# Graph attention on one core: two heads' target rows by VectorE turns and DMA, and their maxima a slot sooner

## What is computed

```python
xl = (x @ W).reshape(B, N, H, F)
asrc = jnp.einsum('bnhf,hf->bnh', xl, a_src)
adst = jnp.einsum('bnhf,hf->bnh', xl, a_dst)
e = jax.nn.leaky_relu(asrc[:, :, None, :] + adst[:, None, :, :], NEG_SLOPE)
e = jnp.where(mask[..., None], e, NEG_INF)
attn = jax.nn.softmax(e, axis=1)
out = jnp.einsum('bsdh,bshf->bdhf', attn, xl)
```

## Time and profile before

| | |
|---|---|
| median of 3 runs | 887.39 us (885.66 to 888.89) |
| the profiled execution | 883.62 us |
| its span, first to last instruction | 881.7 us |
| PE busy | 839.4 us (95%) |
| DVE busy | 745.3 us (85%) |
| ACT busy | 692.9 us (79%) |
| POOL busy | 277.0 us (31%) |
| mean granted clock of TensorE | 0.992 |

### The profile page before, as it was taken

How to read it: one execution, slowest core, us unless ns; L and a number is a source line. 1 busy time by engine, 2 the same in 40 slices (tenths; PEclk the granted TensorE clock), 3 DMA queues, 4 the chain that set the end, 5 groups by cost and what they waited for, 6 DMA issues and landing times.

```text
span 881.7 us, 17000 instructions
## 1 busy us (share of the span) xinstructions
PE 839.4 (95%) x5996; PEld 788.6 (89%) x5996; DVE 745.3 (85%) x1922; ACT 692.9 (79%) x1302; POOL 277.0 (31%) x244
## 2 busy tenths in 40 slices
PE   6798989999999999999999999999999999999896
PEld 4688879999999999999999999899999999889675
DVE  6868797979798888979888896988889798897766
ACT  2677869788796978879697887969788796979563
POOL 0002020233343333334333333433333343334222
PEclk9899999999999999999999999999999999999999
DMA  9123131322313131231423123042312301200002
GB/s 250 55 73 73 48 96 50 96 49 55 93 47 97 68 101 50 70 96 32 93 70 99 49 57 111 26 98 72 96 49 56 106 33 25 72 1 2 24 1 72
DMA packets 100379, 59.81 MB, mean 68 GB/s; under 512 B 66244, under 2 KB 84804, under 8 KB 100296
## 3 DMA queue, kind: packets, MB, share of 16 engines
q1 hardware_dynamic: 100296, 58.73, 24.6%
HBM read 41.82 MB, written 8.50 MB: 57 GB/s over the span
## 4 chain that ended last, share of the span: by engine, by line
PE 75%; DVE 11%; ACT 8%; issue 3%; another core or an unknown queue 0%; POOL 0%; DMA 0%; SPq 0%; POOLq 0%; DVEq 0%; ACTq 0%
PE bUU L558 19%; PE bUU L580 11%; PE bUU L569 10%; PE bG L652 10%; PE bG L670 9%; PE bG L640 4%; PE bB L518 3%; DVE junk L1010 3%; PE bUU L548 2%; ACT att L787 2%; DVE att L1010 2%; PE bG L667 2%; DVE att L1057 1%; PE bA L518 1%; ACT att L802 1%
## 5 line engine op out<-in xcount | busy, mean ns | idle before, releaser
L558 PE MATMUL bUU<-val,att 128*128 128x129 f32 x2048 | 249.5, 275 | 1.3 <-DVE att L1061 1.3
L558 PEld LDWEIGHTS bUU<-val,att 128*128 128x128 f32 x2048 | 240.2, 192 | 2.9 <-issue 1.9
L1061 DVE SCALAR_TENSOR_TENSOR att<-mask_n,att 128x2048 f32<-128x2048 bf16 x64 | 148.5, 2320 | 74.8 <-ACT att L802 69.8
L787 ACT ACTIVATE att<-bB,val 128x512 f32<-128x512 f32 x320 | 204.1, 716 | 5.2 <-PE bB L518 5.2
L802 ACT ACTIVATE att<-att 128x2048 f32<-128x2048 f32 x64 | 123.7, 1933 | 0.6
L426 POOL TENSOR_SCALAR var_eps<-moments 128x4 f32<-128x4 f32 x29 | 29.9, 1032 | 299.1 <-DVE moments L1103 299.1
L1010 DVE CUSTOM_DVE_ANT_0 junk<-mask_t,a_rows,val 128x512 bf16<-128x512 bf16 x168 | 121.8, 778 | 0.0
L569 PE MATMUL bUU<-val,att 128*128 128x257 f32 x480 | 113.1, 385 | 5.1 <-DVE att L1057 4.0
L580 PE MATMUL bUU<-val3s,att 128*128 128x256 f32 x480 | 108.3, 379 | 0.2 <-DVE res L1091 0.2
L1010 DVE CUSTOM_DVE_ANT_0 junk<-mask_t,bA,val 128x512 bf16<-128x512 bf16 x152 | 104.1, 740 | 4.2 <-PE bA L518 4.2
L569 PEld LDWEIGHTS bUU<-val,att 128*128 128x128 f32 x480 | 87.7, 190 | 21.9 <-DVE att L1057 5.4
(11 more groups left out here) (128 smaller groups left out, 1690.5 us busy)
## 6 DMA issues: line engine op xcount, KB each, us to landing
adj_in<-in_adj_dram SPq DMA_DIRECT2D x16, 1024.0 KB, 5.8
a_rows<-a_rows_dram SPq DMA_DIRECT2D x56, 256.0 KB, 3.8
x_in<-in_x_dram SPq DMA_DIRECT2D x16, 512.0 KB, 6.7
out_dram<-act SPq DMA_DIRECT2D x14, 512.0 KB, 2.9
mask_t<-mask_n SPq DMA_TRANSPOSE x64, 2.5
a_rows_dram<-val SPq DMA_DIRECT2D x56, 2.0 KB
att<-in_L_gnn_W_dram SPq DMA_DIRECT2D x4, 128.0 KB, 3.3
val<-in_L_gnn_W_dram SPq DMA_DIRECT2D x1, 512.0 KB, 7.4
```

The lines of the kernel that those rows point to most:

```text
L558: ins = nc.tensor.matmul(to[:, (d % 2) * FX:(d % 2 + 1) * FX], p[:, s, d * P:(d + 1) * P], val1[u.batch % 2][:, s, u.index // 2, values], ...
L787: nc.scalar.activation(p[:, b], bB[:], ACT.Prelu, bias=a_col(u, b), alpha=SLOPE)\
L1061: nc.vector.scalar_tensor_tensor(flat(p), mask_n[u.batch % 3][:, 0:NB * N], BIG, flat(p), ALU.add, ALU.min)\
```

## The change

Four things are changed, all for the heads 2 and 3 of batches 2 to 15 (28 heads):

- Their targets' terms no longer pass through TensorE and `bB`. VectorE writes them to every eighth column of `b_wide` (128x32), turns that in 32x32 blocks into `b_turned`, and SP stores the turned rows to DRAM and reads them back as a row onto 128 partitions (`spread_targets`): head 2's into `a_rows[:, 3]`, free once head 3's source row has been copied to `bA`, head 3's into a new tile `b_rows`. ScalarE's `leaky` reads these rows in SBUF.
- VectorE also turns the sources' scores of the next batch (`turn_scores`, position 2), and `store_scores` writes runs of 32 elements instead of single ones.
- `tops` and `shifted_targets` of head 2 move from position 2 to position 1, behind `keep_edges` of head 0; those of head 3 from position 3 to position 2.
- GpSimd waits for head 2's new semaphore before `add_bias_2`.

```diff
+            def spread_targets(n, i):
+                sp.wait_ge(b_turned_ready, 2 * (n - 2) + i + 1)
+                if n > 2:
+                    sp.wait_ge(b_spread[i], 16 * (n - 2))
+                sp.dma_start(b_dram[i].rearrange("(b q i) -> q b i", b=NB, i=32),
+                             b_turned[0:P:32 // NB, :]).then_inc(b_stored, 16)
+                sp.wait_ge(b_stored, 16 * (2 * (n - 2) + i + 1))
+                if i == 0:
+                    sp.wait_ge(arow_copied, n - 1)
+                elif n > 2:
+                    sp.wait_ge(leaky_done, (units[SLOTS * (n - 1) + 3 + i].u + 1) * NB)
+                sp.dma_start(b_rows[i], b_dram[i].rearrange("(o n) -> o n", o=1).to_broadcast([P, N]))\
+                    .then_inc(b_spread[i], 16)
...
                     load_x(n + 2)
+                if n >= 2:
+                    spread_targets(n, 0)
                 if 2 <= n + 1 < B:
                     store_scores(n + 1)
+                if n >= 2:
+                    spread_targets(n, 1)
+                if 2 <= n + 1 < B:
                     spread_scores(n + 1)
...
-                    pool.wait_ge(b_t_ready, units[SLOTS * n + 3].r + 1)
+                    if n >= 2:
+                        pool.wait_ge(b_turned_ready, 2 * (n - 2) + 1)
+                    else:
+                        pool.wait_ge(b_t_ready, units[SLOTS * n + 3].r + 1)
                     add_bias_2(n - 1)
...
-                if after and after.row:
+                if after and after.row and not after.targets_by_dma:
                     targets_row(after)
...
-                if u.row:
+                if u.targets_by_dma:
+                    act.wait_ge(b_spread[u.index - 2], 16 * (u.batch - 1))
+                elif u.row:
                     act.wait_ge(brow_done, u.r + 1)
...
+                if u.targets_by_dma:
+                    k = 2 * (u.batch - 2) + u.index - 2
+                    if k:
+                        dve.wait_ge(b_turned_ready, k)
+                    nc.vector.scalar_tensor_tensor(b_wide[:, 0:32:32 // NB], top[u.u % 2][:], TOP, low[:], ALU.subtract,
+                                                   ALU.min, reverse0=True).then_inc(b_wide_ready, 1)
+                    if k:
+                        dve.wait_ge(b_stored, 16 * k)
+                    dve.wait_ge(b_wide_ready, k + 1)
+                    nc.vector.transpose(b_turned[:], b_wide[:]).then_inc(b_turned_ready, 1)
+                    return
...
+            def turn_scores(n):
+                dve.wait_ge(val1_ready, (n + 1) * NB)
+                if n > 2:
+                    dve.wait_ge(a_stored, 16 * H * (n - 2))
+                nc.vector.transpose(scores_t[:], val1[n % 2][:, :, :, HC:HX]).then_inc(scores_turned, 1)
...
+                if n >= 2 and pos in (2, 3):
+                    after = units.get(g + 2) if pos == 2 else None
...
+                if pos == 2 and n + 1 < B:
+                    turn_scores(n + 1)
...
+                if pos == 1 and 2 <= n < B:
+                    tops(units[g + 2])
+                    shifted_targets(units[g + 2])
                 if pos == 1 and 0 <= n - 2 < B:
                     norm_stats(n - 2, 0, res1, res1_done, NB, stats1, moments1)
```

More of the change, by code:

```diff
@@ L36, in __init__ @@
         self.banked = self.by_dma and index == 3
+        self.targets_by_dma = self.by_dma and index >= 2
 def gat_kernel(nc, x, adj, W1, as1, ad1, b1, W2, as2, ad2, b2, W3, a3, out):
@@ L74, in gat_kernel @@
         u.u = i
-    for i, u in enumerate(u for u in units.values() if u.row):
+    for i, u in enumerate(u for u in units.values() if u.row and not u.targets_by_dma):
         u.r = i
@@ L148, in gat_kernel @@
         a_rows = sb("a_rows", [P, H, N])
+        b_wide = sb("b_wide", [P, 32])
+        b_turned = sb("b_turned", [P, 32])
+        b_rows = [a_rows[:, H - 1], sb("b_rows", [P, N])[:]]
+        scores_t = sb("scores_t", [P, NB * G * 4])
         act3 = sb("act3", [P, NB, D])
@@ L203, in gat_kernel @@
         a_stored = sem("a_stored")
+        scores_turned = sem("scores_turned")
+        b_wide_ready = sem("b_wide_ready")
+        b_turned_ready = sem("b_turned_ready")
+        b_stored = sem("b_stored")
+        b_spread = [sem(f"b_spread{i}") for i in range(2)]
         a_spread = [sem(f"a_spread{i}") for i in range(H)]
@@ L291, in gat_kernel @@
         a_dram = nc.dram_tensor("a_rows_dram", (H, N), F32).ap()
+        b_dram = nc.dram_tensor("b_rows_dram", (2, N), F32).ap()
         def a_cols(u):
@@ L335, in store_scores @@
             def store_scores(n):
-                sp.wait_ge(val1_ready, (n + 1) * NB)
+                sp.wait_ge(scores_turned, n - 1)
                 for h in range(H):
@@ L340, in store_scores @@
                         sp.wait_ge(a_spread[h], 16 * (n - 2))
-                    with nc.allow_non_contiguous_dma(reason="columns of scores"):
-                        sp.dma_start(a_dram[h].rearrange("(b p) -> p b", p=P), val1[n % 2][:, :, h // 2, HC + h % 2])\
-                            .then_inc(a_stored, 16)
+                    first = h // 2 * 4 + h % 2
+                    sp.dma_start(a_dram[h].rearrange("(b q i) -> q b i", b=NB, i=32),
+                                 scores_t[first:P:NB * G, :]).then_inc(a_stored, 16)
             def spread_scores(n):
@@ L350, in spread_scores @@
                         if h == H - 1:
-                            sp.wait_ge(arow_copied, n - 2)
+                            sp.wait_ge(leaky_done, (units[SLOTS * (n - 1) + 3].u + 1) * NB)
                         else:
@@ L413, in _ @@
             nc.gpsimd.memset(neg_one[:], -1.0).then_inc(consts, 1)
+            nc.gpsimd.memset(b_wide[:], 0.0).then_inc(consts, 1)
             nc.gpsimd.memset(val2[:, :, DX:DX + 1], 1.0).then_inc(consts, 1)
@@ L419, in _ @@
                                     pattern=[[-1, P]], channel_multiplier=1).then_inc(consts, 1)
-            pool.wait_ge(consts, 8)
+            pool.wait_ge(consts, 9)
             nc.gpsimd.tensor_scalar(ident_big[:], ident[:], BIG, 1.0, ALU.mult, ALU.mult).then_inc(consts, 1)
-            pool.wait_ge(consts, 9)
+            pool.wait_ge(consts, 10)
             def norm_scale(m, which, moments_sem, var_sem, rstd_sem):
@@ L533, in targets_row @@
                 pe.wait_ge(b_t_ready, u.r + 1)
-                before = [v for v in units.values() if v.row and v.r == u.r - 1]
+                before = [v for v in units.values() if v.row and not v.targets_by_dma and v.r == u.r - 1]
                 if before:
@@ L710, in first_heads @@
                     values_1(2, 0)
-            pe.wait_ge(consts, 9)
+            pe.wait_ge(consts, 10)
             spread_weights()
@@ L786, in leaky @@
                     if u.row:
-                        nc.scalar.activation(p[:, b], bB[:], ACT.Prelu, bias=a_col(u, b), alpha=SLOPE)\
+                        nc.scalar.activation(p[:, b], b_rows[u.index - 2] if u.targets_by_dma else bB[:], ACT.Prelu, bias=a_col(u, b), alpha=SLOPE)\
                             .then_inc(leaky_done, 1)
@@ L893, in first_heads @@
                     nc.scalar.copy(w2_hi[:], w2).then_inc(w2_hi_ready, 1)
-            act.wait_ge(consts, 9)
+            act.wait_ge(consts, 10)
             nc.scalar.activation(warm[:], neg_one[:], ACT.Exp).then_inc(warmed, 1)
@@ L1160, in fold_1 @@
             def fold_1():
-                dve.wait_ge(consts, 9)
+                dve.wait_ge(consts, 10)
                 for k in range(KD):
```

## The result

The changed kernel takes **879.56 us** (median of 6 runs, 878.99 to 880.27); the kernel before, beside it, took 886.52 (883.31 to 888.89). The ratio is 0.9927, 95% interval 0.9908 to 0.9946: faster by 0.7%. The profiled execution after took 880.02 us with a span of 878.2, against 883.62 and 881.7.

The account below looks back on a forecast made before the run. TensorE bounds the kernel at 51.05 us per period; afterwards a VectorE and ScalarE loop of 51.39 does. Steady periods +3.7, late copies -2.7, batch 15 +1.4, batch 2 +0.8, end -0.7: +2.5, median 889.9 us, range 881 to 897.

Parts of the forecast that it names:

- the late copies: ScalarE's second copy L855, late in some periods during single-element score stores; expected to go with runs of 32: -2.7 us.
- the loop's size: VectorE's stretch plus ScalarE's part, without TensorE: 47.06 us before, 4.33 added, 51.39 us per period after.
- turns: Three new 128x32 turns per batch on VectorE, two of them waiting: 0.50 us added to the loop, bounds 0.25 to 1.2.
- `low` held: VectorE's `low` of head 3 waits for the whole remainder of GpSimd's addition L452: 0.58 us, bounds 0 to 2.1.
- `leaky` from SBUF: ScalarE reads the targets' row in SBUF, making its `leaky` pair slower: 0.20 us, bounds 0 to 0.4.
- 5.18 us: ScalarE's part of the loop, from head 0's second inverse to head 2's `keep_edges`: `normalize`, second `leaky` pair, two copies, exponentials.
- the end: After the steady periods: batch 15 +1.4 us, less 0.7 taken up by TensorE's wait of 0.73; +0.7 us.
- the collision at 790: In batch 15 GpSimd's addition and normalization collided, 3.44 us against 1.38; its going was counted as 2.06 us less.
- carrying the sum to the median: Profiled execution lay 3.8 us under the median; carried over, +2.5 us turned 887.39 into 889.9 us.
- The loop stays short: Rival: `low` not held and turns at their lower bound, period about 50.6, 879 us; hold alone absent, 882; chance 0.22.
- The late copies stay: Rival: the late copies have another cause and count in full in the loop, 895.0 us; chance 0.18.
- TensorE as the bound: Rival: loop under TensorE's 50.18 us per period, so the full 12.2 us come in, 875 us; chance 0.08.

Follow-up runs that it names:

- e10: Kernel before, with 24 unused transposes of a constant filling TensorE's wait in batch 2: 888.3 us, ratio 1.0022.
- e11: Kernel before with scores turned and stored in runs of 32, plus 24 unused transposes filling TensorE's batch 2 wait: 881.31 us, ratio 0.9952.
- e3: Kernel before, with only the next batch's scores turned by VectorE and stored in runs of 32: 882.04 us, ratio 0.998.
- e1: Changed kernel, with GpSimd's bias addition ahead of its two scale operations in position 2: 873.49 us, ratio 0.9882.
- e5: Changed kernel, with two spreads per batch put back on TensorE, unused (0.87 us of work): 880.98 us.
- e7: Changed kernel, with four unused turns of 128x32 and a wait in position 3, under VectorE's idle time: 880.0 us.
- r0: Changed kernel unaltered, run again as companion of later runs on their chip: 879.63 us, ratio 0.9951 to the kernel before.
- e2: Changed kernel, with ScalarE's second `leaky` pair of head 2 ahead of `normalize` of head 0 in position 3: 868.36 us, ratio 0.9826.
- e6: Changed kernel, with four unused turns of 128x32 and a wait in position 2, inside VectorE's stretch of the loop: 886.96 us.
- e9: Kernel before, with head 2's second `leaky` pair ahead of head 0's `normalize` on ScalarE in position 3: 883.73 us, ratio 1.0018.
- e8: Changed kernel, with scores not turned but stored as single elements behind head 3's row: 878.88 us, ratio 0.9954.

## Why the prediction was wrong

**Right.** The mechanism as a whole: TensorE gives up the pace to a loop of VectorE and ScalarE; TensorE waits a little, before layer 2's `attend`; VectorE's idle time is one block of about 5 us (4.84); `low` of head 3 is held by the addition (0.61 us); the rows by DMA come in time; the late copies go; periods are even. Also batch 2, +1.1 against +0.8.

**Wrong: the loop's size.** The prediction had 47.06 + 4.33 = 51.39 us. The trace has 45.92 us for VectorE's stretch (head 2's `keep_edges`, 444.48 - 50.92 = 393.56, to the second inverse, 439.48) and 5.00 for ScalarE (439.48 to 444.48), 50.92 together. Term by term:

| term | forecast | measured |
|---|---|---|
| turns | 0.50 | 0.77 (0.41 and 0.52 from `b_wide` to the next work, less twice the 0.08 that followed `b_t`) |
| `low` held | 0.58 | 0.44 |
| VectorE's stretch in all | 46.01 | 45.92 |
| `leaky` from SBUF | +0.20 | +0.09 (pair 1.23 against 1.14) |
| two copies of layer-2 values | 0.80, inside the 5.18 | 0.52 |
| ScalarE's part in all | 5.38 | 5.00 |

The step that failed most is "5.18 us", the part of the loop that was taken whole from the old trace as ScalarE's work. It held a wait. Before, the two copies start at 388.66 and the exponentials 0.80 us later; after, 0.52 us later. The second copy and the exponentials before, and TensorE, which finished the values for this copy only then:

```profile
389.19 0.38 ACT L855 COPY val<-bG 128x258 f32<-128x258 f32 x1
389.46 1.91 ACT L802 ACTIVATE att<-att 128x2048 f32<-128x2048 f32 x1
```
```profile
388.75 0.28 PE L652 MATMUL bG<-w_lo,y_hi 128*128 128x258 f32 x1
388.87 0.28 PE L652 MATMUL bG<-w_hi,y_lo 128*128 128x258 f32 x1
388.99 1.95 PE L558 MATMUL bUU<-val,att 128*128 128x129 f32 x16
```

The last of the L652 ends near 389.15, which is where the second copy could begin. So TensorE, which the loop was meant to leave out, was in it for 0.28 us, too short to be listed as idle time. After the change TensorE is ahead and the wait is gone. With the smaller `leaky` that is 0.38 us. In VectorE's stretch the errors of the turns and the hold nearly cancel (+0.27 and -0.14), and 0.22 us less than the sum remain. They are an error of reading: the work ahead of an idle place was counted to the end of its last instruction, where an instruction that follows without a wait starts some 0.08 us before that end. So `b_t` at 379.21 was counted with 0.16 us instead of 0.08, head 0's first inverse with 0.16 instead of 0.08, and head 2's two, up to the next start, with 0.25 instead of 0.15. That is 0.26 us; what is left nearly cancels, with `low` of layer 2 0.20 us longer beside GpSimd's normalization (L469) as the largest part. In all 0.47 us per period, over eleven periods 5.2 us: the forecast of +0.34 against TensorE's old 51.05 became -0.13.

On the hold, the Trainium skill (SBUF — State Buffer, Who interferes with whom) says that the later of two such instructions waits for the whole of the earlier. By that rule, the trace agrees here: `low` ended 0.02 us after L486. The meeting too was as forecast, with 0.59 us of the addition left when `low` began (434.77 to 435.36) against 0.58. The term was too large because the whole remainder was added: `low` did not need its 0.17 us once more behind the addition, 0.15 of them passed inside the hold. The rows had this: `keep_edges` at 79.43 took 4.20 us, 0.14 less than the 2.05 left of the addition and its own 2.29.

**Wrong: the end.** Forecast +0.7, measured -1.36. I counted the collision at 790 that goes (3.44 against 1.38, and it did), and missed another: before, a layer-2 `keep_edges` ran beside GpSimd's normalization and its addition. VectorE before and after:

```profile
814.18 4.77 DVE L1057 SCALAR_TENSOR_TENSOR att<-mask_n,att 128x1024 f32<-128x1024 bf16 x2
```
```profile
813.15 2.35 DVE L1107 SCALAR_TENSOR_TENSOR att<-mask_n,att 128x1024 f32<-128x1024 bf16 x2
816.48 2.44 POOL L486 TENSOR_TENSOR x_in<-x_in,bias 128x1024 f32<-128x1024 f32 x1
```

Before, the addition started at 815.21, inside the 4.77 us. After, it starts (last row) 1 us behind the end of `keep_edges`. That is 2.4 us, about the whole of the miss of 2.1; that it lies on the path to the end was not tested, so the cause of this part stays open.

**Wrong: carrying the sum to the median.** For the profiled execution the forecast was 886.1 and 880.02 was measured, 6.1 too much. The other 4.2 us come from adding the 3.8 us by which the median of before lay above its profile, and from a median after that lies 0.5 below its profile. No longer execution of that set was traced, so what the 3.8 us were is not known for certain. The later runs show two things that vary in the kernel before and can make it up: late copies (e10 against e11), and falls of the clock in batch 2 (e3, e10). The two traces of the changed kernel show neither. But the clock can fall there too. TensorE's wait in that place is 2.29 us instead of 3.14, the same in e1, e5 and e7, and in these three traces the clock fell behind it for some 3 us. TensorE in e7:

```profile
126.00:130.00 4.00, 4.00 (x23) 4.00 (x22) 3.83 (x13) 1.98 (x4) 2.57 (x2) 0.57 0.25 62
```

It cost nothing: batch 2 took 50.09 us in e7 and 50.08 in r0, at full clock. In r0 TensorE waits 1.75 us for a copy some 10 us later, and in e7 this wait is gone. So what the changed kernel is spared is the loss, not the fall; and a mean clock of 0.991, as two of its own twelve runs have, goes with its two fastest times (878.58 and 878.85). e11, the kernel before without both, took 881.31 us; the changed one, in other sets of runs, 879.6. By the traces, the eleven steady periods give 1.25 of these 1.7 us, and batch 2 (+1.08) and the end (-1.5) nearly cancel.

**The rivals.** "The loop stays short", 879 to 882 us, gave the right time with a partly wrong reason, so by luck: the hold was there (0.44 us) and the turns cost 0.77 us, not their lower bound. "The late copies stay" did not come true: with stores in runs none is late. TensorE as the bound came only with e2. How much of the 7 us each part brought differs from set to set of runs, because the kernel before differs: 886.5, 884.5, 884.1, 882.5 and 885.6 us in five sets of companion runs.

## What to carry to other kernels

When an engine has been taken from its place as the bound, build the next loop from the trace, and look into each of its segments for short waits on the old bound: 0.28 us between two copies was worth 3 us of forecast. Once a loop of two engines sets the pace, the same microsecond costs everything or nothing by where it stands (e6, e7), and an order edit that was worth nothing before can be the largest gain (e9, e2: 11 us). A median that lies well above its profiled execution says that something happens in some runs only; find it before it is carried over as a constant.

## What the runs showed of the hardware

- A 3.14 us wait of TensorE was followed in some executions by a granted clock of 0.50 for some 6 us and 2.6 us of lost time (batch 2 51.57 in e3, 51.69 in e9, against 48.98), in others by none; filled to 0.52 us, no mean clock of 22 executions was under 0.992. After 2.29 us the clock fell in the traces of e1, e5 and e7 (0.57 over 4 us) and in the six others with this wait not, and there the fall cost no time.
- Two kernels that differ in the form of the DMA stores (2048 stores of 4 bytes, against runs of 32 elements with one turn more) took 888.3 and 881.3 us. Beside the element stores a fetch of 8 KB of instructions took 6.6 us, against 0.3 to 0.8 us in e11, and ScalarE stood still for 1.75 to 2.86 us with no engine behind it; a row of 256 KB read beside them landed after 9.5 us instead of 3.2 (e8).
- A turn of 128x32 in f32 takes 0.18 to 0.21 us, follows another in 0.10 to 0.14, and starts 0.27 us after the start of an instruction of 0.17 us that it depends on.
- The chain store of 2 KB, read onto 128 partitions: 1.6 us from the store's issue to the read's, 3.2 us more to landing.
